# New places for the side operations of a kernel of two Mamba layers and two attentions

## What is computed

```python
def mamba(h, ...):                       # L0 and L2, DI = 512, 16 states
    xm, z = split(h @ W_in, 2)
    xm = silu(causal_conv4(xm) + conv_b)
    dtr, Bm, Cm = split(xm @ W_xp, [64, 80])
    dt = softplus(dtr @ W_dt + b_dt)
    # over the 256 positions:
    #   hst = hst * exp(dt * A) + (dt * x) * B ;  y = sum over states of hst * C
    return ((y + xm * D) * silu(z)) @ W_out

x = x + gate * mamba(layernorm(x) * (1 + scale) + shift)[inv_perm]   # L0, tokens permuted
x = x + silu(film(layernorm(softmax_attention(layernorm(x))))) @ W   # L1, 16 heads of 16
x = x + gate * mamba(layernorm(x) * (1 + scale) + shift)             # L2
x = x + silu(film(layernorm(linear_attention(layernorm(x))))) @ W    # L3, masked keys
```

## Time and profile before

| | us |
|---|---|
| median of 3 runs | 5344.82 |
| lowest, highest | 5313.51, 5346.1 |
| the profiled execution | 5308.23 |
| its span | 5306.5 |

### The profile page before, as it was taken

The page is one execution under the profiler, slowest core; times in us unless marked ns, Lnnn a source line. Parts: engine busy times, 40 slices in busy tenths (PEclk is TensorE's granted clock), DMA queues, the critical chain, the costliest instruction groups (busy, mean ns, idle before and its releaser), DMA issues.

```text
span 5306.5 us, 54840 instructions
## 1 busy us (share of the span) xinstructions
PE 4408.0 (83%) x16792; PEld 2421.4 (46%) x16792; DVE 4653.1 (88%) x4552; ACT 3277.8 (62%) x5574; POOL 4054.0 (76%) x2840
## 2 busy tenths in 40 slices
...
GB/s 147 236 218 126 201 232 233 238 222 240 256 219 232 221 243 230 236 261 217 237 223 233 230 241 261 217 240 216 241 233 240 246 233 250 214 242 184 105 220 64
DMA packets 355050, 1164.53 MB, mean 219 GB/s; under 512 B 39347, under 2 KB 79330, under 8 KB 354758
## 3 DMA queue, kind: packets, MB, share of 16 engines
...
...
## 4 chain that ended last, share of the span: by engine, by line
DVE 41%; PE 28%; issue 12%; ACT 9%; DMA 5%; POOL 4%; SPq 1%; ACTq 0%; DVEq 0%; POOLq 0%
DVE hw L1234 20%; DVE ps L1220 8%; PE ps L1121 5%; PE ps L1472 5%; PE ps L1499 4%; PE ps L893 3%; PE ps L1334 3%; DVE mx L1592 3%; ACT pts L1567 2%; DMA bs<-bc_scratch 2%; ACT da L1170 2%; POOL hw L1252 2%; DMA xhat<-in_x 2%; DVE stats L819 1%; DVE u L1073 1%
## 5 line engine op out<-in xcount | busy, mean ns | idle before, releaser
L1252 POOL TENSOR_TENSOR hw<-hw,cs 128x1024 f32<-128x1024 f32 x1024 | 2414.3, 2358 | 664.2 <-DVE hw L1234 620.4
L1234 DVE TENSOR_TENSOR_SCAN hw<-da,ps 128x1024 f32<-128x1024 f32 x1024 | 2335.1, 2280 | 29.0 <-PE ps L1121 6.2
L1170 ACT ACTIVATE da<-dt,a_neg 128x510 f32<-128x510 f32 x2048 | 1326.1, 710 | 233.8 <-DVE hw L1234 230.1
L1259 POOL TENSOR_TENSOR hw<-hw 128x512 f32<-128x512 f32 x1024 | 1298.5, 1268 | 69.5
L1220 DVE TENSOR_TENSOR ps<-ps,bs 128x1024 f32<-128x1024 f32 x1024 | 1256.6, 1227 | 59.4 <-DMA bs<-bc_scratch 18.8
L1121 PE MATMUL ps<-hw,ident 128*128 128x512 f32 x2048 | 1128.9, 662 | 116.1 <-POOL hw L1259 115.8
L1121 PEld LDWEIGHTS ps<-hw,ident 128*128 128x128 f32 x2048 | 403.2, 209 | 574.8 <-issue 320.2
L893 PE MATMUL ps<-hT,w_in 128*128 128x512 f32 x1024 | 531.4, 650 | 86.4 <-DVE dt L1081 69.4
L1567 ACT ACTIVATE pts<-ps 128x512 f32<-128x512 f32 x512 | 280.2, 593 | 381.4 <-PE ps L1499 381.3
L1592 DVE TENSOR_REDUCE mx<-ps 128x2 f32<-128x512 f32 x512 | 329.7, 683 | 151.6 <-PE ps L1472 151.6
L770 ACT ACT_TABLE_LOAD x321 | 411.8, 1283 | 28.9 <-DVE x_c L1782 23.3
...
## 6 DMA issues: line engine op xcount, KB each, us to landing
bs<-bc_scratch SPq DMA_DIRECT2D x1024, 512.0 KB, 5.0
cs<-bc_scratch SPq DMA_DIRECT2D x1024, 512.0 KB, 3.8
...
```

The lines of the kernel that those rows point to most:

```text
L1170: ins = nc.scalar.activation(da[q % (AHEAD + 1)][:, k, :, 1:S], dt_[:, c, :].rearrange("p (b s) -> p b s", b=GB)[:, :, 1:S], ACT.Exp, scal ...
L1234: nc.vector.tensor_tensor_scan(tile[:, :, :].rearrange("p n t -> p (n t)"), da[s % (AHEAD + 1)][:, :, :, :].rearrange("p n b s -> p (n b s)"),
L1252: nc.gpsimd.tensor_tensor(tile[:, :, :], tile[:, :, :], cs[s % C_RING][:, :, :], ALU.mult)\
L1259: nc.gpsimd.tensor_tensor(tile[:, 0, :], tile[:, 0, :], tile[:, 1, :], ALU.add)\
```

## The change

All numbers of `PLACES` are replaced; `AT`, `PLAN`, the pieces, their instructions, waits, banks and buffers stay. The core of the diff, one engine's list a line, for what the prediction speaks of:

```diff
     "even": {
         "attn_b": {
-            "dve": [-67.333, -34.667, 5.553, 5.777, 6.11, 6.22, 6.464, 6.598, 6.732, 6.866, 7.165, 7.498, 7.665,
-                   7.832, 8.553, 8.777, 9.055, 9.11, 9.165, 9.275, 17.066, 17.132, 17.198, 17.264, 19.464,
-                   19.598],
+            "dve": [-67.333, -34.667, 5.165, 5.498, 5.665, 5.832, 6.165, 6.553, 6.777, 7.082, 7.165, 7.248,
+                   7.665, 8.165, 8.498, 8.665, 9.082, 9.165, 9.248, 9.553, 17.464, 17.598, 17.732, 17.866,
+                   20.047, 20.141],
...
         "front1": {
-            "pe": [20.467, 20.633, 20.967, 21.133, 21.8, 25.9, 26.2, 26.82, 31.8],
+            "pe": [20.633, 20.967, 21.633, 21.967, 23.633, 26.729, 26.843, 27.071, 28.014],
...
         "lin_a": {
-            "pe": [18.1, 19.8, 20.8, 23.633, 23.967, 24.633, 24.967, 25.6, 26.66, 26.98, 27.14],
+            "pe": [16.8, 17.7, 19.1, 23.967, 24.633, 24.967, 25.9, 26.614, 26.957, 27.186, 27.443],
...
         "mid1": {
-            "dve": [30.165, 31.165],
+            "dve": [30.553, 30.777],
...
     "odd": {
         "attn_a": {
-            "pe": [6.8, 8.8, 9.05, 9.45, 9.6, 9.75, 9.9, 10.05, 10.2, 10.35, 11.8, 12.4, 12.7, 12.8, 12.9,
-                   13.1, 13.2, 13.411, 13.522, 13.633, 13.744, 13.856, 13.967, 14.078, 15.411, 15.522, 15.633,
-                   15.744, 15.856, 15.967, 16.078, 16.189, 17.7, 18.1, 18.767, 19.033],
-            "dve": [5.832, 5.916, 11.027, 11.055, 11.082, 11.11, 11.165, 11.248, 11.275, 11.303, 11.397, 11.464,
-                   11.531, 11.598, 11.665, 11.732, 11.799, 11.866, 11.933, 12.11, 18.066, 18.132, 18.198,
-                   18.264, 20.665, 22.066],
+            "pe": [6.8, 7.55, 7.8, 9.5, 9.7, 9.9, 10.3, 10.767, 11.033, 11.5, 11.7, 11.9, 12.1, 12.5, 12.9,
+                   13.411, 13.522, 13.744, 13.856, 13.967, 14.078, 14.189, 15.633, 15.8, 15.967, 16.133, 17.45,
+                   17.6, 17.75, 17.9, 18.05, 18.2, 18.35, 18.9, 20.5, 24.55],
+            "dve": [5.832, 5.916, 11.414, 11.665, 11.749, 11.832, 11.916, 12.027, 12.055, 12.082, 12.11, 12.137,
+                   12.193, 12.248, 12.275, 12.303, 12.464, 12.598, 12.732, 12.866, 19.11, 19.165, 19.22,
+                   19.275, 21.665, 23.082],
...
         "front0": {
-            "pe": [23.633, 23.967, 24.8, 25.54, 25.78, 26.02, 27.7, 27.9, 29.175],
-            "act": [20.3, 22.6, 23.65, 23.8, 23.95, 25.267, 25.433, 27.5, 27.7, 27.9, 29.85],
-            "dve": [22.132, 22.198, 26.665, 27.165, 27.665, 28.665, 28.832, 29.165, 31.83],
+            "pe": [24.8, 25.05, 25.7, 26.1, 26.66, 26.98, 27.14, 27.8, 28.05],
+            "act": [20.35, 23.8, 24.35, 24.6, 25.433, 25.767, 26.433, 28.3, 28.5, 28.7, 29.767],
+            "dve": [23.165, 23.247, 27.11, 27.22, 28.497, 28.665, 28.832, 29.22, 31.83],
...
         "mid0": {
-            "act": [27.3, 28.6, 29.35, 29.6],
-            "dve": [31.11, 31.22],
+            "act": [29.267, 29.433, 29.6, 29.933],
+            "dve": [31.58, 32.08],
```

More of the change, by code:

```diff
@@ L201 @@
         "front0": {
[L202 to L206, removed]
+            "pe": [4.8, 6.8, 15.633, 15.967, 22.55, 22.8, 23.05, 31.633, 31.967],
+            "act": [0.075, 2.7, 6.767, 8.767, 21.6, 23.3, 23.8, 29.433, 29.6, 29.767, 29.933],
+            "dve": [1.665, 2.165, 23.665, 25.11, 25.22, 31.497, 31.663, 31.83, 32.163],
+            "pool": [2.8, 29.3],
+            "sp": [-41.2, -21.6],
         },
         "rest0": {
[L209 to L213, removed]
+            "pe": [-66.667, -33.333, 2.767, 3.033, 5.633, 5.967, 9.9, 16.8],
+            "act": [0.025, 0.05, 2.3, 2.5, 2.9, 6.433, 8.433, 12.6, 29.267],
+            "dve": [1.165, 10.665, 14.665, 31.997],
+            "pool": [2.3, 11.3, 22.217, 22.383],
+            "sp": [-80.4, -60.8],
         },
@@ L217 @@
         "attn_a": {
[3 rows of a table removed]
[L221 to L226, removed]
@@ L243 @@
+            "pool": [21.383, 27.8, 28.75],
+            "sp": [-55.455, -46.545],
         },
         "back0": {
[L245 to L248, removed]
-            "sp": [-2.908, -2.815],
+            "pe": [-64.286, -42.857, -35.714, -28.571, -14.286],
+            "act": [-66.667, -55.556, -22.222, -11.111],
+            "dve": [0.083, 0.165, 0.247, 0.553, 0.665],
@@ L263 @@
-            "sp": [-2.169, -2.077],
+            "pe": [-92.857, -85.714, -78.571, -71.429, -57.143, -50],
+            "act": [-88.889, -77.778, -44.444, -33.333],
+            "dve": [-67.333, -34.667],
+            "pool": [-50, 2.8],
+            "sp": [-19.818, -10.909],
         },
@@ L393 @@
-            "pool": [3.3, 17.8, 19.8],
-            "sp": [-2.723, -2.631],
[3 rows of a table added]
+            "act": [3.544, 3.656, 3.767, 3.989, 6.35, 6.6, 6.85, 7.56, 10.35, 10.6, 10.85, 11.6, 12.2, 12.3,
+                   12.4, 12.5, 12.6, 12.8, 12.9, 13, 15.62, 15.74, 15.86, 15.98, 16.35, 16.6, 16.85, 17.3,
+                   17.7, 17.9, 18.6],
+            "dve": [3.665, 3.833, 7.635, 7.695, 7.756, 7.817, 7.878, 7.939, 8.082, 8.165, 8.456, 8.498, 8.581,
+                   8.623, 8.665, 8.832, 8.916, 8.958, 9.11, 9.22, 17.442, 17.665, 17.777, 17.888, 19.464,
+                   19.598],
@@ L428 @@
-            "pool": [6.925, 13.3, 31.425],
-            "sp": [-2.169, -2.077],
+            "pe": [7.633, 7.729, 7.776, 8.062, 8.11, 8.252, 9.9, 11.5, 12.967, 13.8, 17.6],
+            "act": [7.68, 7.74, 7.8, 7.86, 7.92, 7.98, 8.04, 8.433, 8.767, 12.7, 14.6, 17.5],
+            "dve": [7.513, 7.574, 8.248, 8.372, 8.414, 8.539, 8.707, 8.749, 8.791, 8.874, 10.165, 12.11, 12.22,
+                   16.165, 17.553],
+            "pool": [7.925, 11.8, 30.8],
+            "sp": [-19.818, -10.909],
@@ L437 @@
+            "pool": [2.8, 6.3, 7.675, 7.8],
+            "sp": [-37.636, -28.727],
         },
@@ L460 @@
-            "pool": [21.8, 29.8, 32.05],
-            "sp": [-2.018, -1.909],
+            "pe": [22.8, 23.05, 23.8, 26.767, 27.033, 27.55, 27.8, 28.05, 29.55, 29.8, 30.05],
+            "act": [22.433, 22.767, 23.65, 23.8, 23.95, 27.267, 27.433, 27.6, 27.767, 27.933, 29.433, 29.767],
+            "dve": [21.165, 21.247, 24.497, 24.665, 24.832, 25.165, 26.082, 26.165, 26.247, 26.665, 28.497,
+                   28.665, 28.832, 31.663, 31.997],
+            "pool": [21.383, 29.3, 32.05],
+            "sp": [-11.8, -1.9],
```

262 lines of the change are left out of this document (125 added, 137 removed), and 31 rows, old and new, of the table PLACES.

## The result

The changed kernel takes 5286.99 us (median of 8 runs, 5274.16 to 5298.87), the kernel before 5338.02 beside it: ratio 0.991, 95% interval 0.9893 to 0.9927. A second set on another chip gave 5295.97 against 5331.07, ratio 0.9934, interval 0.9918 to 0.995. So the gain is 35 to 51 us, where 5 us more were forecast: inside the range of 5270 to 5430, but on the other side of no change and beyond what scatters. The profiled execution took 5281.93 us for a span of 5280.2.

A forecast was written before the change was run, and what follows sets the result against it. DVE, busy 88% of the span, was taken as the bound, leaving only its idle time to win. Odd steps -65, their tails +56, even steps +14 summed to +5 us: 5313 profiled, 5350 on the median's scale, range 5270 to 5430.

The forecast's parts named there:

- Waits of `mx` in the repeating steps: Sign of being right: DVE's waits of attention's reductions for their score matmuls fall from 116.5 to about 60 us.
- three joints: Odd step: places left where two reduction pairs stand back to back, 0.62 us of waiting each, 0.95 more at half clock.
- Gain of the odd step's reductions: Odd step, waits at `mx` and `q`: 9.4 us now, 4.4 left; gain 5.0 us, bounds 2 and 7.5.
- Gain of the even step's reductions: Even step: 2.2 us of `mx` waits, scans now at almost every joint; gain 1.0 us, bounds 0 and 2.2.
- Tail of the even step: End of the even step: later PE work makes DVE wait at `lin_a.xo`, `dt0`, `dt1`; loss 2.0 us, bounds 0 and 4.
- Tail of the odd step: Odd step's end into next DBX0: `c2` ends 5.4 us later, delaying slice `bs`; new waits 4.0 us, bounds 0 and 7.
- Other waits of the odd step: Odd step: `front0.st` gains 0.7 us, `qm` loses 0.7; together 0, bounds -0.7 and +1.5.
- One-off steps: Steps outside the repeating ones: chains keep the same links in order; 0 us, bounds -15 and +15 over all.
- The tail holds: Faster rival: both tails cost 1 us, the odd gain is 6; -64 us, so 5281 us; chance 0.20.
- The clock decides: Rival: closer packing puts PE at full clock in the odd step's joints; 37 us less at most, 5332 us; chance 0.06.
- The signs named beforehand: Right if `mx` waits fall to about 60, slice waits reach 30, new x_c, u, dt waits; odd near 159, even 149.

The follow-up runs named there:

- even_new: Kernel before, with the changed places in the step "even" alone; ratio 0.9938 to the kernel before.
- after_nm1_first: Changed kernel, but in the odd step PE issues nm1 ahead of lin_b's transposes and RED11; ratio 0.9933 to the kernel before.
- nm1_qm: Changed kernel with nm1 ahead of RED11 and lin_b's transposes, and lin_b's qm one scan later, qs behind DBX17; ratio 0.9948 to the kernel before.
- lin_k_half: Changed kernel with half the matmuls of the linear attention's k projection left out (computes something else); ratio 0.9916 to the kernel before.
- lin_k_twice: Changed kernel with the matmuls of the linear attention's k projection issued twice; ratio 0.9966 to the kernel before.
- single_new: Kernel before, with the changed places in "first", "second", "last_but_one", "last" and "end" alone; ratio 1.0005 to the kernel before.

## Why the prediction was right or wrong

The sign was lost in the even step: -1.0 for its reductions and +2.0 for its tail made +1.0 us a step, and it measured -2.2, 14 times. even_new, with that table alone, has the gain (0.9938, where the whole has 0.9934 and 0.991). The two terms of the odd step, -5.0 and +4.0, were further off, in opposite directions. Term by term, "us of the sum" being what each error makes over all steps:

- *Waits of `mx` in the repeating steps, 116.5 to about 60:* right, 59.4. In an odd step 59.4 / 13 = 4.6 us are left, where 4.4 were taken; but there are 5 waits in it (65 / 13), where three joints were counted.
- *Gain of the odd step's reductions, -5.0 each:* the largest single error. It set 9.4 us of `mx` and `q` against 4.4. The 2.3 us of `q` came from one step; on average it was 10.7 / 13 = 0.8. And `q` was costed at nothing afterwards, because `Lb.k` moved behind `nm1`; but `nm1` itself went behind RED11 and lin_b's transposes, and `q` waits 29.0 / 13 = 2.2. Timeline of PE and of DVE, changed kernel, as the earlier trace rows:
```profile
1782.87 1.90 PE L1120 MATMUL ps<-hw,ident 128*128 128x512 f32 x2
1784.57 0.64 PE L1481 MATMUL ps<-ident,mx 128*128 128x128 f32 x4
```
```profile
1785.24 0.69 DVE L1598 TENSOR_TENSOR q<-q,ps 128x512 f32<-128x512 f32 x1 [2.15 <-PE ps L1481]
```
  On average `mx` went from (116.5 - 14 x 1.8) / 13 = 7.0 to 4.6 us (1.8 is its mean in an even step) and `q` from 0.8 to 2.2: 7.8 became 6.8, -1.0 instead of -5.0. This error makes the forecast too fast, by 52 us of the sum.
- Deeper than that, the step "a wait removed is time gained" doesn't hold in an odd step: after_nm1_first and nm1_qm took 21 of `q`'s 29 us away for nothing. That PE is behind there fits lin_k_half and lin_k_twice.
- *Gain of the even step's reductions, -1.0 (0 to 2.2):* too small. The waits (2.2 us in the step of the earlier trace rows, 1.8 on average) went wholly, and scan 12 comes 2.1 to 2.6 us earlier. Some -2.2 in 14 places, 17 us more than taken. By the sorted steps above most of it is the half-clock stretch that went, for which the forecast had no term in the even step.
- *Tail of the even step, +2.0:* wrong in its main part. There is no wait at x_c: PE ends `out` 130.4 us behind the first scan (130.5 before), just as DVE gets to it. `dt0` and `dt1` do wait 0.25 and 1.37 instead of 1.14, about as said, +0.5. From scan 12 on the step is 0.4 us longer, not 2.0. That is 22 us of the sum.
- *Tail of the odd step, +4.0:* right in kind, a third in size. `c2` was to end 5.4 us later. Chain of one of the changed kernel's odd steps, as the earlier trace rows:
```profile
1836.01 3.62 PE L863 MATMUL ps<-onehot,xhat 128*128 128x256 f32 x16
...
1851.56 1.88 PE L892 MATMUL ps<-hT,w_in 128*128 128x512 f32 x4
1853.27 1.02 PE L1120 MATMUL ps<-hw,ident 128*128 128x512 f32 x2
...
1856.10 3.58 PE L901 MATMUL ps<-u,taps 128*128 128x512 f32 x8
```
```profile
1864.00 0.59 ACT L1026 ACTIVATE xd<-ps 96x512 f32<-96x512 f32 x1 [0.44 <-PE ps L916]
```
```profile
1871.89 1.23 DVE L1219 TENSOR_TENSOR ps<-ps,bs 128x1024 f32<-128x1024 f32 x1 [1.69 <-DMA bs<-bc_scratch]
```
  The means over the 13 odd steps, in us behind the step's first scan, before and after: `h0` begins at 118.7 and 121.4, `c2` ends at 143.3 and 145.0, `xd` at 148.6 and 150.0, and DBX0 starts at 156.7 and 158.0. The second profiles of both kernels have the same, +2.9, +1.9, +1.6 and +1.2. So this chain is as late as the odd step is longer. `h0` came 2.7 us later where 3.5 were added. What failed is the row of PE behind it: it was put at 3.7 + 6 + 16.8 = 26.5 us from the start of `h0` to the end of `c2`, where it had taken 24.6 and took 23.7. Part of this is that whole durations were added, while a group of matmuls begins before the one ahead of it ends: above, `m3` lasts 1.88 us and RED25 begins 1.71 after its start. (A single step misleads here: in the short one shown `h0` begins at 119.1, in the long one of the earlier trace rows at 1854.81 - 1734.3 = 120.5, which would make it earlier.) The 7.6 us from `xd` to DBX0 held (7.3). DVE waits 2.4 us for the slice at the even step's first product instead of 1.0, +1.5 in 14 places: 35 us less than taken.
- *Other waits of the odd step, 0:* the residual `gate` +0.5, `u` +0.3, `xhat` and the product `yg` -0.3 each, about right in sum. But 0.9 us of the odd step's +1.3 stand in no named wait: gaps under 0.15 us and instructions of DVE that overlap less. *One-off steps, 0 within 15:* single_new 1.0005, right in sum for their own tables; in the whole change the profiles have -15 us there, -7 of it in the odd step after "second", which got no term.
- *The rivals.* "The tail holds" (5281) came nearest in time, by luck: its gain of 6 in the odd step's reductions was 1, and the even step's gain was larger than it said. "The clock decides", at 6%, named the right quantity for the wrong step: the half-clock stretch went from the even step, while in the odd one, where the rival put its gain, half-clock time grew from 11.6 to 15.0 us.
- *The signs named beforehand.* `mx` near 60 us, the slice at 30 or more, new waits at `u` and `dt`, and odd steps near 159 all came; of the waits only that at x_c didn't. Even steps measured 146.6 where 149 stood, inside the 3 us allowed. But 14 x 2.4 = 34 us is most of the error: a sign that allows 3 us a step can't tell +5 us from -35.

The sum as measured in the profiles: even steps 14 x -2.2, odd steps 13 x +1.2 from one pair of profiles, where the forecast had +14 and 13 x -5 + 56 = -9. Both signs were the wrong way round; the one-off steps make the other -15.
